# The product with V issued as two products of 256 queries, one behind each half of an attention slot, where another slot follows

## The chip, the cores and the metric

One core of one Trainium2 chip runs the whole program. The metric is the device time of one execution in microseconds; lower is better. The kernel before took 3469.8 us, the median of three runs between 3466.66 and 3474.9 us. Engines: TensorE (PE, its weight loads PEld), VectorE (DVE), ScalarE (ACT), GpSimd (POOL), SyncE (SP, which issues the DMAs).

## The reference

Four transformer-like layers follow each other on `x` of 4 batches x 1024 rows x 256 features, all in float32. What matters here is the self-attention of layer 0 and of layer 2, with 16 heads of 16 features:

```
s = einsum('bqhd,bkhd->bhqk', q, k) * scale      # layer 0: masked by blocks; layer 2: all keys
a = softmax(s, axis=-1)
out = einsum('bhqk,bkhd->bqhd', a, v)
```

Layers 0 and 2 go on with an output projection, cross attention over 77 context rows and an MLP; layer 1 is a mixture of three experts, layer 3 another cross attention, computed together with layer 2.

## The kernel before

Two program regions hold a self-attention: `FEWR` for layer 0 (two key tiles of 128 matter, so `per` = 2; a general region `GENR` is built beside it and not run with these inputs) and `L2R` for layer 2 (`per` = 8 key tiles). A region works on blocks: one block is one batch `b`, one group `g` of four heads (`j` = 0 to 3, one in each 32 rows of the array) and one half `qh` of the queries (512). There are 32 blocks in a region: 64 slots in layer 0 and 256 in layer 2.

A **slot** is one step of that pipeline for one key tile. For slot `t`, TensorE's program (`slot`, line 1149) has two halves, and each half has, before the change:

- the scores of slot `t` for two heads, written to two PSUM banks (`("sc", t, j)`: heads 0 and 1 in the first half, 2 and 3 in the second). In layer 2 (`by_parts`) a score takes three matmuls of 512 columns on 32 rows of the array: two parts of q, and the row of subtracted maxima (`max_rows`);
- the *fills*: scores of a later block, the other way round, for the other two heads, into two more banks, from which VectorE takes the maxima (`max_halves`, L1680). Heads 2 and 3 in the first half, 0 and 1 in the second, so that the four groups of 32 rows are all in use;
- behind the first half alone, the product with V of slot `t`-1 (`pv`, line 1099): four matmuls of 512 columns, 128 rows x 32 array columns each, that accumulate over a block's key tiles in the bank `ACC`. It waits for all four exponentials of slot `t`-1. Below, a slot's product is numbered by its key tile `i` (0 to 7 in layer 2).

The trace and the instruction order name a matmul `ps<-moving,stationary`: `ps<-q_blocks,k_groups` are the score parts, `ps<-max_rows,max_rows_ones` their third step, `ps<-k_groups,q_blocks` the fills, `ps<-big,probs` the product with V (a float32 matmul is two instructions in the trace, one in the order).

ScalarE turns each score bank into exponentials (L2024, `big<-ps`), and with that frees the bank. Seven banks form a **ring** (`take`, `R.freed`): the scores, fills and transposes take them in the order in which TensorE's program names them, and TensorE waits until the engine that reads the bank's entry seven places earlier has freed it. A slot takes 8 (four scores, four fills), so the fill of head 3 in the next slot's first half gets the bank of this slot's score of head 2.

Once in a block, behind a slot's second half, come four transposes of maxima (`nms`, L1180; in layer 2 in the slot whose product is `i` = 5) and four of the accumulated output (`tails`, L1168; in the slot whose product is `i` = 0). The product with `i` = 0 starts a new sum in `ACC`, and so first waits until ScalarE has copied the old one out (`R.acc`, L1999, `o_T<-ps`).

A planner (`overlapped`) puts the slots and all other work of the layer (projections, cross attention, MLP) into one order, by costs and due times worked out when the program is built. That order is fixed, and every engine keeps it. In layer 2's first 200 us hardly anything but slots is ready; later a slot usually has other matmuls on both sides.

Of the kernel before, what the change touches and what calls it, by code (L numbers as in the profile page):

```python
# [16 lines left out]
NB, SEQ, D = 4, 1024, 256  # L17
# [5 lines left out]
HALF = 512  # L23
# [42 lines left out]
def pixart_kernel(nc, io):  # L66
    ctx = ExitStack()
    with ctx:
# [51 lines left out]
        PS = ctx.enter_context(nc.psum_tensor("ps", [P, 8, HALF], F32))  # L120
# [11 lines left out]
        PB = BIG[:, 8192:12288].rearrange("p (a j n) -> p a j n", a=2, j=HG)  # L132
# [138 lines left out]
        ACC = 7  # L271

        class Region:
# [3 lines left out]
            def __init__(self, name, l, few, overlap, rows_first):  # L277
                self.name, self.l, self.few, self.rope, self.masked = name, l, few, l == 0, l == 0 and not few
                self.keys = list(range(NT - LIVE, NT)) if few else list(range(NT))
                self.per = len(self.keys)  # L280
                self.total = NG * NH * self.per
                self.split = l == 2
                self.lead = self.per + (3 if self.split else 2)
                self.rows_first = rows_first
                self.crosses = (1,) if l == 0 else (1, 2)
                self.share = 12.0 if few else 3.4
                self.order = overlapped(self) if overlap else sequential(self)
                self.number, self.lns, self.turns, self.loads, self.adds = {}, {}, [], {}, {}
                self.parted = [tok[1:] for tok in self.order if tok[0] == "qk"] if self.split else []
                self.cross_products = [tok for tok in self.order if tok[0] == "cp"]  # L290
                self.kv_users = [tok[2:] for tok in self.order if tok[0] == "load" and tok[1] == "k"]
                self.last = {}
                for tok in self.order:
                    if tok[0] in ("oP", "cp"):
                        self.last[tok[:3]] = tok
                    elif tok[0] == "m2":
                        self.last[tok[:2]] = tok
                self.cross_outs = [tok for tok in self.order if tok[0] == "ct"]
                n = 0
                for tok in self.order:  # L300
                    for key in self.entries(tok):
                        self.number[key] = n
                        n += 1
                    if tok[0] == "lnA":
                        self.lns[tok[1:]] = len(self.lns)
                    if tok[0] == "qk" and self.rope:
                        self.turns.append(tok[1:])
                    if tok[0] == "load":
                        self.loads[tok[1:]] = sum(1 for k in self.loads if k[0] == tok[1])
                    for add in self.bias_adds(tok):  # L310
                        self.adds[add] = len(self.adds)
                self.ring_full, self.ring_free = (sems(name + side, "0 1 2 3 4 5 6") for side in ("ring_full", "ring_free"))
                self.pv, self.acc, self.nm, self.rec, self.crec = sems(name, "pv_done acc_out max_done recip cross_recip")
                self.ln_st, self.ln_mv, self.ln_ep, self.ln_rs, self.ln_norm = sems(name + "ln_", "stats mean_var eps rstd rows")
                if not self.split:
                    self.rp_f, self.qe, self.ke = sems(name, "turned groups_act groups_dve")
                    self.x_in, self.x_g, self.cs, self.ones = sems(name, "wco_in wco_gated cos_sin_in v_ones")
                else:
                    self.ba_g = sems(name, "bias_o_gated")[0]
                    self.part_hi, self.nm_f, self.nm_h = sems(name, "part_hi max_f32 max_hi")  # L320
                    self.part_out = sems(name, "parts_out_0 parts_out_1")
                    self.q_in = sems(name, "q_block_in_0 q_block_in_1 q_block_in_2")
                    self.kg_in = sems(name, "k_group_in_0 k_group_in_1")
                self.xt = XTP if overlap else XT
                if few:
                    self.t12, self.fr, self.cos, self.sin = KE[:, 0:2, 0:HALF], KE[:, 2:4, 0:HALF], VS[:, 1152:1664], VS[:, 1664:2176]
                else:
                    pairs = PR[:, 0:2048].rearrange("p (x a n) -> p x a n", x=2, a=2)
                    self.t12, self.fr, self.cos, self.sin = pairs[:, 0], pairs[:, 1], OT[:, 0:HALF], OT[:, HALF:SEQ]
                self.affine = (0, 1, 2, None) if l == 0 else (4, 5, 6, 7)  # L330
                self.eps = (1e-5, 1e-5, 1e-5, None) if l == 0 else (1e-6, 1e-6, 1e-6, 1e-5)
                self.o_in, self.o_g, self.m_in, self.m_g, self.w1_in = sems(name, "wo_in wo_gated w2_in w2_gated w1_in")
                self.k_in = sems(name, "kv_in_first kv_in_second")
                self.bm_g, self.biased = sems(name, "bias_m_gated biased")
# [639 lines left out]
        def _(pe):  # L974
            def mm(out, lhsT, rhs, first=True, last=True):
                return pe.matmul(out, lhsT, rhs, start=first, stop=last)  # L976
# [3 lines left out]
            for kt in range(KT):  # L980
                last = pe.transpose(PS[:, 0, kt * NB:(kt + 1) * NB], condR[:, kt * P:(kt + 1) * P], ident[0:NB, 0:NB])
# [72 lines left out]
            def region_pe(R):  # L1054
# [41 lines left out]
                                last = mm(PS[:, bank, q * P:(q + 1) * P], MQ[:, qh * 4 + q, kt * P:(kt + 1) * P], bigI[:, :], False, q == 3)  # L1096
                        done(last, ("sc", t, j))

                def pv(t):
                    b, g, qh, i = R.at(t)  # L1100
                    for j in range(HG):
                        pe.wait_ge(*R.freed(("sc", t, j)))
                    if i == 0:
                        if t:
                            pe.wait_ge(R.acc, t // R.per)
                        if R.few:
                            pe.wait_ge(*R.freed(("v", b, 0, 0)))
                        else:
                            for k in range(2):
                                pe.wait_ge(*R.freed(("v", b, g // 2, k)))  # L1110
                    for j in range(HG):
                        h = 8 * (g // 2) + 2 * j + g % 2
                        last = mm(PS[32 * j:32 * j + 32, ACC, :], R.v_tile(b, i, h), PB[:, t % 2, j, :], i == 0, i == R.per - 1)
                    last.then_inc(R.pv, 1)

                def by_parts(t, f, half):
                    keys, stationary, moving = [], [], []
# [30 lines left out]

                def slot(tok):
                    _, score, fills, product, tails, nms = tok  # L1150
                    for half in range(2):
                        if R.split:
                            by_parts(score, fills, half)
                            if half == 0 and product is not None:
                                pv(product)
                            continue
                        if score is not None:
                            scores(score, half)
                        for key in R.fills(fills, half):
                            fill(key)  # L1160
                        if half == 0 and product is not None:
                            pv(product)
                    for q in tails:
                        pe.wait_ge(R.acc, q + 1)
                        bank = take(("tail", q))
                        for i in range(4):
                            c = (q % 2) * HALF + i * P
                            last = pe.transpose(PS[:, bank, i * P:(i + 1) * P], OT[:, c:c + P], ident[:, :])  # L1168
                        done(last, ("tail", q))
                    for q in nms:  # L1170
                        if R.few:
                            pe.wait_ge(*R.freed(("max", q, R.per - 1, 1)))
                        else:
                            pe.wait_ge(R.nm, q + 1)
                        b, g, qh = R.block(q)
                        bank = take(("nm", q))
                        for i in range(4):
                            qt = 4 * qh + i
                            rows = NM[:, q % 2, i:i + P] if R.split else NM[:, 2 * qh + g % 2, qt:qt + P]
                            last = pe.transpose(PS[:, bank, i * P:(i + 1) * P], rows, ident[:, :])  # L1180
                        done(last, ("nm", q))
# [17 lines left out]
                for tok in R.order:  # L1199
# [5 lines left out]
                    elif kind == "v":  # L1205
                        b, m = tok[1:]
                        for hf in range(NH):
                            wait_turned("lnT", 0, b, hf)
                        for i in range(1 if R.few else 2):
# [5 lines left out]
                            else:  # L1215
                                for u in range(4):
                                    t = 4 * i + u
# [1084 lines left out]
```

## Time and profile before

| | us |
|---|---|
| median of three runs | 3469.8 |
| the profiled execution | 3466.48 |
| its span on the core | 3464.7 |
| PE busy in the span | 3150.7 (91%) |
| DVE busy | 1823.9 (53%) |
| ACT busy | 1464.3 (42%) |

The span is the time from the first to the last instruction; 1.8 us of the execution lie around it. Matmuls on different rows or columns of the array overlap, so PE's busy time is the time in which at least one was under way, and a matmul's duration runs on while the next has already begun. The distance between starts is therefore what the sums below use. Idle time is written in brackets behind a row, with the instruction whose end closed it.

### The profile page before, as it was taken

How to read it: one execution, taken by the hardware profiler on the slowest of the kernel's cores; microseconds unless marked ns; L12 is line 12 of the kernel's file. 1: busy time of each engine (PE TensorE's matmuls, PEld its weight loads, DVE VectorE, ACT ScalarE, POOL GpSimd, SP SyncE). 2: the span in 40 equal slices, each digit the busy share in tenths (PEclk: the TensorE clock that was granted, in tenths of full speed). 3: DMA queues.
4: the chain of work that ended last, by engine and by line, in shares of the span. 5: the costliest groups of instructions: out<-in, count | busy, mean ns of one | idle time of the engine just before them, and what ended most of it. 6: DMA issues, size and time to landing. Idle time of an engine off the chain costs nothing.

```text
span 3464.7 us, 51568 instructions
## 1 busy us (share of the span) xinstructions
PE 3150.7 (91%) x20564; PEld 1858.1 (54%) x20564; DVE 1823.9 (53%) x3812; ACT 1464.3 (42%) x2645; POOL 257.2 (7%) x278
## 2 busy tenths in 40 slices
PE   6899999999889999998488989999999999999887
PEld 3555666656576656665234445454454545554464
DVE  4876554562412332323377765757757577557343
ACT  0343444444312222221046645555456555565433
POOL 1100010010100000000100001001100101001010
PEclk9998999999889999999689989999999999999899
DMA  5200000003000000000420020001200000000000
GB/s 168 91 1 6 8 21 1 15 14 96 16 23 0 1 0 1 1 0 5 143 67 32 26 75 24 15 20 44 86 13 22 28 28 25 13 28 31 1 1 13
DMA packets 78707, 104.29 MB, mean 30 GB/s; under 512 B 18688, under 2 KB 52208, under 8 KB 78204
## 3 DMA queue, kind: packets, MB, share of 16 engines
q1 hardware_dynamic: 78468, 100.93, 9.0%
q8 instruction: 171, 2.80, 0.3%
q14 instruction: 68, 0.56, 0.1%
HBM read 72.05 MB, written 28.86 MB: 29 GB/s over the span
## 4 chain that ended last, share of the span: by engine, by line
PE 80%; DVE 9%; ACT 4%; DMA 2%; issue 2%; SPq 1%; POOL 1%; DVEq 0%; ACTq 0%; POOLq 0%
PE ps L976 73%; PE ps L1189 3%; DVE max_halves L1680 2%; ACT big L2024 2%; DMA k_parts<-qk_parts 1%; PE ps L1316 1%; PE ps L1180 1%; DVE row_max_cross L1846 1%; DMA q_parts<-qk_parts 1%; PE ps L1168 1%; DVE xn_tok L1752 1%; DVE bn_stats L1716 1%; ACT probs L2083 1%; SPq L877 1%; DVE bn_stats L1739 1%
## 5 line engine op out<-in xcount | busy, mean ns | idle before, releaser
L2024 ACT ACTIVATE big<-ps 128x512 f32<-128x512 f32 x1280 | 692.7, 595 | 668.3 <-PE ps L976 667.8
L1680 DVE TENSOR_REDUCE max_halves<-ps 128x1 f32<-128x512 f32 x1024 | 650.3, 683 | 239.9 <-PE ps L976 232.4
L976 PE MATMUL ps<-k_groups,q_blocks 32*128 32x512 f32 x2048 | 449.4, 464 | 89.8 <-DVE qk_parts L1815 33.8
L976 PE MATMUL ps<-q_blocks,k_groups 32*128 32x512 f32 x2048 | 423.4, 468 | 4.0 <-DVE qk_parts L1815 2.0
L976 PE MATMUL ps<-big,probs 128*32 128x512 f32 (+1 forms) x2688 | 383.6, 613 | 12.3 <-ACT big L2024 5.8
L976 PE MATMUL ps<-weights_mlp,big 128*128 128x256 f32 (+1 forms) x1248 | 333.5, 419 | 2.5 <-ACT big L2095 2.5
L976 PEld LDWEIGHTS ps<-q_blocks,k_groups 32*128 32x128 f32 x2048 | 175.9, 187 | 297.2 <-issue 282.9
L976 PEld LDWEIGHTS ps<-weights_mlp,big 128*128 128x128 f32 x1248 | 234.0, 190 | 83.6 <-issue 57.9
L976 PEld LDWEIGHTS ps<-k_groups,q_blocks 32*128 32x128 f32 x2048 | 188.8, 190 | 158.4 <-ACT big L2024 55.6
L1722 DVE TENSOR_TENSOR x_tok<-ps,x_tok 128x512 f32<-128x512 f32 x112 | 77.2, 690 | 312.1 <-PE ps L976 311.9
L2083 ACT ACTIVATE probs<-ps 77x512 f32<-77x512 f32 x384 | 196.2, 591 | 96.0 <-PE ps L976 95.7
L976 PE MATMUL ps<-x_T,weights_mlp 128*128 128x256 f32 x1024 | 231.4, 385 | 2.3 <-ACT x_T L2046 2.3
L976 PE MATMUL ps<-big 32*128 32x256 f32 (+2 forms) x1664 | 224.3, 492 | 10.0 <-DVE row_max L1677 4.3
L1677 DVE TENSOR_REDUCE row_max<-ps 128x2 f32<-128x512 f32 x256 | 164.6, 684 | 103.3 <-PE ps L976 103.1
L976 PEld LDWEIGHTS ps<-x_T,weights_mlp 128*128 128x128 f32 x1024 | 195.3, 193 | 34.6 <-ACT x_T L2046 4.9
L976 PE MATMUL ps<-max_rows,max_rows_ones 32*128 32x512 f32 x1024 | 204.5, 398 | 0.0
L976 PEld LDWEIGHTS ps<-big 32*128 32x128 f32 (+1 forms) x1664 | 142.3, 193 | 108.6 <-issue 80.6
L976 PE MATMUL ps<-weights,x_T 128*128 128x256 f32 x640 | 164.9, 412 | 2.9 <-ACT x_T L1999 2.9
L1846 DVE TENSOR_REDUCE row_max_cross<-ps 128x4 f32<-128x308 f32 x384 | 155.0, 469 | 17.2 <-PE ps L976 16.0
L2095 ACT ACTIVATE big<-ps,mlp_b 128x256 f32<-128x256 f32 x256 | 106.8, 470 | 128.0 <-PE ps L976 127.8
L976 PE MATMUL ps<-big,k_v_cross 32*77 32x512 f32 (+1 forms) x832 | 156.0, 627 | 3.2 <-DVE big L1852 2.2
L2238 POOL TENSOR_SCALAR eps_tile<-mean_var 128x4 f32<-128x4 f32 x56 | 13.3, 237 | 1845.4 <-DVE mean_var L1745 1845.3
(233 smaller groups left out, 3970.7 us busy)
## 6 DMA issues: line engine op xcount, KB each, us to landing
q_blocks<-q_parts SPq DMA_DIRECT2D x64, 256.0 KB
q_parts<-qk_parts SPq DMA_DIRECT2D x48, 256.0 KB
k_parts<-qk_parts SPq DMA_DIRECT2D x32, 256.0 KB
k_groups<-k_parts SPq DMA_DIRECT2D x16, 512.0 KB
weights_mlp<-in_L_xcond_mlp_W SPq DMA_DIRECT2D x5, 1024.0 KB, 5.3
weights_mlp<-in_L_xcond_W_mlp SPq DMA_DIRECT2D x5, 1024.0 KB, 5.1
x_tok<-in_x SPq DMA_DIRECT2D x4, 1024.0 KB, 9.6
out_y<-x_tok SPq DMA_DIRECT2D x8, 512.0 KB, 3.2
```

Of the source, the lines that this page charges most:

```text
L877: sp.dma_start(dst, STG[:, n % STAGES, part, :].bitcast(F32)).then_inc(R.part_out[n % STAGES], 16)
L976: return pe.matmul(out, lhsT, rhs, start=first, stop=last)
L1168: last = pe.transpose(PS[:, bank, i * P:(i + 1) * P], OT[:, c:c + P], ident[:, :])
L1180: last = pe.transpose(PS[:, bank, i * P:(i + 1) * P], rows, ident[:, :])
L1189: last = pe.transpose(PS[:, banks[ft], (t % 4) * P:(t % 4 + 1) * P], rows[:, t, ft * P:(ft + 1) * P], ident[:, :])
L1677: dve.tensor_reduce(NM[:, 2 * qh + e, c:c + 2], PS[:, bank, :].rearrange("p (t n) -> p t n", t=2), AX.X, ALU.max, negate=True).then_inc(R. ...
L1680: dve.tensor_reduce(NMP[:, e, j, qt, hf:hf + 1], PS[:, bank, :], AX.X, ALU.max, negate=True).then_inc(R.frees(key), 1)
L1722: dve.tensor_tensor(x, PS[:, R.bank(key), :], x, ALU.add).then_inc(R.frees(key), 1)
L1846: dve.tensor_reduce(dst, src, AX.X, ALU.max, negate=True).then_inc(R.frees(key), 1)
L2024: act.activation(PB[:, score % 2, j, :], PS[:, R.bank(key), :], ACT.Exp, scale=SCALE).then_inc(R.frees(key), 1)
L2083: act.activation(PC[0:NC, j, :], PS[0:NC, R.bank(key), :], ACT.Exp, scale=SCALE).then_inc(R.frees(key), 1)
L2095: last = act.activation(HT[hf][:, m, :], PS[:, R.bank(key), i % 2 * D:(i % 2 + 1) * D], ACT.Gelu_apprx_tanh, bias=B1[:, 0 if R.l == 0 else ...
```

## The change

In `Region.__init__` the set `followed` collects the slots behind which the fixed order places another slot directly (tokens that cost TensorE nothing are skipped). In such a slot, if its product isn't the block's first (`product % R.per > 0`), `slot` now issues the product as two: queries 0 to 255 behind the first half's scores and fills, queries 256 to 511 behind the second half's. Each has four matmuls of 256 columns with the same weights. The signal that a product is done (`R.pv`) and the end of a block's sum go with the second. All other slots keep the one product of 512.

```
--- before.py
+++ after.py
@@ -288,6 +288,8 @@
                 self.number, self.lns, self.turns, self.loads, self.adds = {}, {}, [], {}, {}
                 self.parted = [tok[1:] for tok in self.order if tok[0] == "qk"] if self.split else []
                 self.cross_products = [tok for tok in self.order if tok[0] == "cp"]
+                placed = [tok for tok in self.order if cost(self, tok)]
+                self.followed = {tok for tok, after in zip(placed, placed[1:]) if tok[0] == after[0] == "slot"}
                 self.kv_users = [tok[2:] for tok in self.order if tok[0] == "load" and tok[1] == "k"]
                 self.last = {}
                 for tok in self.order:
@@ -1096,7 +1098,7 @@
                                 last = mm(PS[:, bank, q * P:(q + 1) * P], MQ[:, qh * 4 + q, kt * P:(kt + 1) * P], bigI[:, :], False, q == 3)
                         done(last, ("sc", t, j))
 
-                def pv(t):
+                def pv(t, columns, closes):
                     b, g, qh, i = R.at(t)
                     for j in range(HG):
                         pe.wait_ge(*R.freed(("sc", t, j)))
@@ -1110,8 +1112,9 @@
                                 pe.wait_ge(*R.freed(("v", b, g // 2, k)))
                     for j in range(HG):
                         h = 8 * (g // 2) + 2 * j + g % 2
-                        last = mm(PS[32 * j:32 * j + 32, ACC, :], R.v_tile(b, i, h), PB[:, t % 2, j, :], i == 0, i == R.per - 1)
-                    last.then_inc(R.pv, 1)
+                        last = mm(PS[32 * j:32 * j + 32, ACC, columns], R.v_tile(b, i, h), PB[:, t % 2, j, columns], i == 0, closes and i == R.per - 1)
+                    if closes:
+                        last.then_inc(R.pv, 1)
 
                 def by_parts(t, f, half):
                     keys, stationary, moving = [], [], []
@@ -1148,18 +1151,19 @@
 
                 def slot(tok):
                     _, score, fills, product, tails, nms = tok
+                    halved = tok in R.followed and product is not None and product % R.per > 0
                     for half in range(2):
                         if R.split:
                             by_parts(score, fills, half)
-                            if half == 0 and product is not None:
-                                pv(product)
-                            continue
-                        if score is not None:
-                            scores(score, half)
-                        for key in R.fills(fills, half):
-                            fill(key)
-                        if half == 0 and product is not None:
-                            pv(product)
+                        else:
+                            if score is not None:
+                                scores(score, half)
+                            for key in R.fills(fills, half):
+                                fill(key)
+                        if halved:
+                            pv(product, slice(half * D, half * D + D), half == 1)
+                        elif product is not None and half == 0:
+                            pv(product, slice(0, HALF), True)
                     for q in tails:
                         pe.wait_ge(R.acc, q + 1)
                         bank = take(("tail", q))
```

74 of the 320 slots that run are concerned: 6 in layer 0 (products 3, 5, 7, 9, 11, 13 of its 64), and 68 in layer 2 (numbered 0 to 255): 48 in the first stretch (1 to 30 and 33 to 55, without the products with `i` = 0), six pairs (59 and 60, 110 and 111, 124 and 125, 171 and 172, 187 and 188, 228 and 229) and 242 to 247, 251 and 252 at the end, where no fills are left. The order on VectorE, ScalarE, GpSimd and SyncE is the same as before.

TensorE in layer 2, from product 1 (`big,probs`) to product 2, before: the second half of one slot (five rows), then directly the first half of the next (five rows).

```order
L976 MATMUL ps<-big,probs 32x512 x4
L976 MATMUL ps<-q_blocks,k_groups 128x512 x2
L976 MATMUL ps<-k_groups,q_blocks 128x512 x2
L976 MATMUL ps<-q_blocks,k_groups 128x512 x2
L976 MATMUL ps<-k_groups,q_blocks 128x512 x2
L976 MATMUL ps<-max_rows,max_rows_ones 128x512 x2
L976 MATMUL ps<-q_blocks,k_groups 128x512 x2
L976 MATMUL ps<-k_groups,q_blocks 128x512 x2
L976 MATMUL ps<-q_blocks,k_groups 128x512 x2
L976 MATMUL ps<-k_groups,q_blocks 128x512 x2
L976 MATMUL ps<-max_rows,max_rows_ones 128x512 x2
L976 MATMUL ps<-big,probs 32x512 x4
```

And now; the last five rows are again the next slot's first half, behind which product 2's first part comes.

```order
L978 MATMUL ps<-big,probs 32x256 x4
L978 MATMUL ps<-q_blocks,k_groups 128x512 x2
L978 MATMUL ps<-k_groups,q_blocks 128x512 x2
L978 MATMUL ps<-q_blocks,k_groups 128x512 x2
L978 MATMUL ps<-k_groups,q_blocks 128x512 x2
L978 MATMUL ps<-max_rows,max_rows_ones 128x512 x2
L978 MATMUL ps<-big,probs 32x256 x4
L978 MATMUL ps<-q_blocks,k_groups 128x512 x2
L978 MATMUL ps<-k_groups,q_blocks 128x512 x2
L978 MATMUL ps<-q_blocks,k_groups 128x512 x2
L978 MATMUL ps<-k_groups,q_blocks 128x512 x2
L978 MATMUL ps<-max_rows,max_rows_ones 128x512 x2
```

Half of the product has moved behind the second half's matmuls, between them and the next slot's first scores.

TensorE in layer 0, from product 3 to product 4 (`big` 128x512 the scores, 128x256 the fills, `row_max` the transposes of maxima), before:

```order
L976 MATMUL ps<-big,probs 32x512 x4
L976 MATMUL ps<-big 128x512 x2
L976 MATMUL ps<-big 128x256 x4
L1180 MATMUL ps<-ident,row_max 128x128 x4
L976 MATMUL ps<-big 128x512 x2
L976 MATMUL ps<-big 128x256 x4
L976 MATMUL ps<-big,probs 32x512 x4
```

And now:

```order
L978 MATMUL ps<-big,probs 32x256 x4
L978 MATMUL ps<-big 128x512 x2
L978 MATMUL ps<-big 128x256 x4
L978 MATMUL ps<-big,probs 32x256 x4
L1184 MATMUL ps<-ident,row_max 128x128 x4
L978 MATMUL ps<-big 128x512 x2
L978 MATMUL ps<-big 128x256 x4
L978 MATMUL ps<-big,probs 32x512 x4
```

Here the moved part stands between the second half and the four transposes.

## Rows read from the trace of the kernel before

**Rows 1.** The page: engines' busy time, and the chain that ended last by engine.

```profile
PE 3150.7 (91%) x20564; PEld 1858.1 (54%) x20564; DVE 1823.9 (53%) x3812; ACT 1464.3 (42%) x2645; POOL 257.2 (7%) x278
PE 80%; DVE 9%; ACT 4%; DMA 2%; issue 2%; SPq 1%; POOL 1%; DVEq 0%; ACTq 0%; POOLq 0%
```

**Rows 2.** The chain in layer 2's first stretch (start us, us, what).

```profile
1813.58 0.61 ACT big L2024
1814.19 0.04 issue
1814.23 2.65 PE ps L976 x23
...
1816.90 0.61 ACT big L2024
```

**Rows 3.** Waits of PE, 1780 to 1980 us (total us, times, longest).

```profile
PE ps L976 <- ACT big L2024: 18.1, 40, 0.5
```

**Rows 4.** Timeline of one slot (start us, us, what, idle before).

```profile
1851.07 0.50 PE L976 MATMUL ps<-q_blocks,k_groups 32*128 32x512 f32 x2
...
1851.64 0.40 PE L976 MATMUL ps<-max_rows,max_rows_ones 32*128 32x512 f32 x2
...
1851.65 0.39 PE L976 MATMUL ps<-q_blocks,k_groups 32*128 32x512 f32 x2
1851.85 2.71 DVE L1680 TENSOR_REDUCE max_halves<-ps 128x1 f32<-128x512 f32 x4 [0.60 <-PE ps L976]
...
1852.07 1.08 ACT L2024 ACTIVATE big<-ps 128x512 f32<-128x512 f32 x2 [0.71 <-PE ps L976]
...
1852.72 0.49 PE L976 MATMUL ps<-k_groups,q_blocks 32*128 32x512 f32 x1 [0.45 <-ACT big L2024]
...
1853.39 1.07 PE L976 MATMUL ps<-big,probs 128*32 128x512 f32 x8
...
1854.38 0.50 PE L976 MATMUL ps<-q_blocks,k_groups 32*128 32x512 f32 x2
```

**Rows 5.** Timeline where the transposes of maxima follow (products 21 and 22).

```profile
1847.27 0.50 PE L976 MATMUL ps<-q_blocks,k_groups 32*128 32x512 f32 x2
...
1848.18 0.66 PE L1180 MATMUL ps<-ident,row_max 128*128 128x128 f32 x4
...
1848.76 0.50 PE L976 MATMUL ps<-q_blocks,k_groups 32*128 32x512 f32 x2
...
1850.07 1.07 PE L976 MATMUL ps<-big,probs 128*32 128x512 f32 x8
```

**Rows 6.** Timeline where a block ends (product 24 waits for `o_T`).

```profile
1856.35 0.61 ACT L1999 ACTIVATE o_T<-ps 128x512 f32<-128x512 f32 x1
...
1857.32 1.07 PE L976 MATMUL ps<-big,probs 128*32 128x512 f32 x8 [0.56 <-ACT o_T L1999]
```

**Rows 7.** Groups of PE by shape (count, busy us, mean ns).

```profile
L976 PE MATMUL ps<-big,probs 128*32 128x512 f32 x2560 | 353.2, 624 | 11.8 <-ACT big L2024 5.8 <-ACT o_T L1999 5.3 <-DVE max_halves L1680 0.5
...
L976 PE MATMUL ps<-weights_mlp,big 128*128 128x256 f32 x1024 | 228.0, 381 | 2.5 <-ACT big L2095 2.5
...
L976 PE MATMUL ps<-weights_mlp,big 128*128 128x512 f32 x224 | 105.5, 592 | 0.0
```

**Rows 8.** Layer 0, timeline of PE from product 9's second half on.

```profile
193.05 1.15 PE L976 MATMUL ps<-big 32*128 32x512 f32 x12
194.13 0.66 PE L1180 MATMUL ps<-ident,row_max 128*128 128x128 f32 x4
...
196.40 0.64 PE L976 MATMUL ps<-big,probs 128*32 128x512 f32 x4
```

**Rows 9.** Layer 2's end, no fills: products 244 and 245.

```profile
3205.55 1.07 PE L976 MATMUL ps<-big,probs 128*32 128x512 f32 x8 [0.80 <-ACT big L2024]
...
3208.78 0.64 PE L976 MATMUL ps<-big,probs 128*32 128x512 f32 x4 [1.25 <-ACT big L2024]
```

**Rows 10.** Busy us of each engine, 1776 to 1976 us, granted clock behind POOL.

```profile
1776.00:1976.00 200.00, 178.19 (x1662) 76.58 (x1656) 150.99 (x249) 128.61 (x239) 2.94 (x14) 1.00 0.10 35
```

## The prediction

> **What bounds the kernel now.** I read the page's busy times and chain first. TensorE is busy 91% of the span and holds 80% of the chain, VectorE 53% and 9% [rows 1]: what counts is where TensorE itself waits inside the slots. The chain in layer 2's first stretch shows that wait as a cycle: 2.65 us of matmuls, then one 0.61 us exponential, with period 1816.90 - 1813.58 = 3.32 us, one slot [rows 2]. TensorE's waits give the amount, 18.1 us in 40 waits of 0.45 on `big` from ScalarE [rows 3]. The timeline of one slot says why [rows 4]. With the start of a slot's second half (1851.07) as zero:
>
> - its third score step starts at 0.57, and the next slot's first half follows at 0.58, beside it;
> - ScalarE begins the exponential of head 2's score at 1.00, as soon as that is complete;
> - at 1.65 the bank comes free, and the fill of head 3, which takes that bank, starts behind 0.45 us of idle. The other matmuls of the half are queued behind it;
> - the product starts at 2.32 (0.67 later) and holds TensorE for 0.99, until the next second half at 3.31.
>
> So between second half and product 1.74 us pass, with little to do before the bank is free, while the product comes only after that. ScalarE itself is not full: it sat idle 0.71 before that exponential, and VectorE 0.60 before its maxima [rows 4]; over 200 us of this stretch they are busy 128.6 and 151.0 us [rows 10].
>
> **The change part by part.** It adds, in 74 slots, four matmuls of 256 columns with their loads and the repeated waits, and moves half of the product behind the second half.
>
> *A half product.* The trace has no product of 256 columns. A float32 matmul of 256 columns takes 381 ns against 592 for 512 on the full array [rows 7], so 256 columns are worth 0.21 per pass; the product has two passes in which its four matmuls overlap, and 0.99 - 2 x 0.21 = 0.57. Bounds: 0.50 (exactly half) and 0.99 (no column saved). I take 0.57, since the product's own mean of 624 ns lies by the 592 of the same width.
>
> *The lost overlap.* Scores can't start beside the third step any more when a product stands between. From a second half's start to transposes behind it 1848.18 - 1847.27 = 0.91 pass [rows 5], against 0.58 to a next half; I take 0.91 before each half product. The step before the product fits it: 0.67 after the late fill, of which two steps. The second part's repeated waits were met before the first part, and lie in that same 0.91.
>
> *The plain slot.* Second half and half product 0.91 + 0.57 = 1.48; then the next first half starts. Its fourth matmul needs the bank freed at 1.65, 0.17 later. A first step is followed by the second after 1.65 - 1.48 + 0.67 = 0.84 at most until the product, less than the 0.91 that the half takes anyway, so the wait is absorbed. The same holds for the other half, whose last fill needs head 0's exponential: the distances are the same. A slot lasts 2 x 1.48 = 2.96 instead of 3.31: 0.35 less. ScalarE's two pairs (1.08 each) fit. VectorE's four maxima, 2.71 with the last one's end [rows 4], fit less easily; they are the first cover to go (below).
>
> *The slots at a block's ends.* Before the slot with `i` = 1 stands an unhalved one; only its own first part is shorter: 0.42. Behind the halved `i` = 5 come the transposes, 1848.76 - 1848.18 = 0.58, which filled the wait already; from second half to product it was 1850.07 - 1847.27 = 2.80 [rows 5], so 3.79 with the product. Now 0.91 + 0.57 + 0.58 + 0.91 + 0.57 = 3.54: 0.25 less. Behind `i` = 7, the next product waits for ScalarE's copy of the sum: 1857.32 - 1854.38 = 2.94 after the second half [rows 4, 6]. Now TensorE is there after 0.91 + 0.57 + 0.91 = 2.39, and waits as long as before. The copy itself comes behind four exponentials, at 1.97 [rows 6], when the second part, over at 1.48, is long done. So nothing is won or lost there. A block with seven halved slots gains 0.42 + 4 x 0.35 + 0.25 + 0.35 = 2.42.
>
> *The sum.* First stretch: six blocks of seven, 14.5, and one of six (0.42 + 1.40 + 0.25, less 0.07 as its last part stands before an unhalved product: 2.39 against 2.32), 2.0: 16.5. Six pairs: 0.42 + 0.35 each, 4.6; behind three an unhalved plain slot (0.07 each), behind two the transposes (2.97 against 2.80, 0.17 each), behind one a block's start: less 0.55, so 4.1. Slots without fills have period 3208.78 - 3205.55 = 3.23, bound by the exponentials that the product waits for, 1.25 of idle [rows 9]; now the matmuls' 2.96: eight slots, 2 x 0.42 + 6 x 0.27 - 0.07 = 2.4. Layer 0: a half slot takes 194.13 - 193.05 = 1.08, and second half to product 3.35 [rows 8]; with the part in it 1.08 + 0.57 + 0.58 + 1.08 = 3.31, hence 0.42 + 0.04 = 0.46, times six 2.8. Together 25.8, say 26 us. All of it lies on TensorE, and the order behind it is fixed.
>
> Nothing else is late: the maxima, the loads and ScalarE's order are untouched; the finished signal of a product moves back by 1.0 us or so, and the exponential that needs it (the buffer of two slots before) starts only after the next half is through.
>
> The profiled execution took 3466.5 (span 3464.7), 3.3 below the median; 3466.5 - 26 = 3440.5, and on the median's scale **3444 us**.
>
> A rule speaks against the change: the Trainium skill, TensorEngine Tiling (Array Packing), section Key Properties, says that changing the tiling mode drains TensorE, and scores (32 rows) and products (32 columns) are two modes. The trace agrees: 0.91 instead of 0.58 where another shape follows [rows 4, 5]. If those drains came on top, 74 x 0.33 = 24 us of the gain would go, by the rows; but most of each lies in the wait.
>
> **The rivals.**
>
> *The halves cost nearly what the whole did.* If the passes are set by the four column strips' loads and starts and not by columns, each half costs up to 0.99, a plain slot 2 x (0.91 + 0.99) = 3.80, and the change is slower. Some 140 half products lie on the path (those behind `i` = 7 are covered), 0.42 more each: 59 us, 26 - 59 = 33 us slower, **3503**. It decides from a half product of about 0.75 on, where 26 us are used up. For it: eight loads and starts are issued again, and nothing so narrow and short was profiled. Against: 256 columns save 0.21 in every full-array row [rows 7].
>
> *VectorE becomes the bound.* Four maxima need about 2.5 to 2.7 of a 2.96 slot, and once in a block the minima and the normalisation stand in between. If the banks then come late from VectorE, the slot stays at about 3.13 and half is won: 13 us, **3457**. For it: 151 of 200 us busy [rows 10]. Against: VectorE has a whole slot to free a bank, ScalarE half of one.
>
> *The stretch's gain is given back.* If what follows at 1976 waits for transfers or GpSimd rather than for TensorE, 16.5 us are lost and 9 stay: **3460**. Against: later stages' chain is TensorE as well [rows 1].
>
> That the change touches too little is no rival of its own: 74 slots are named by the order, and 18.1 us of idle stand in one stretch alone [rows 3].
>
> **How the numbers follow.** The forecast has 0.73, spread by the half product (0.50 gives 10 us more, 0.65 gives 12 less) between 3433 and 3457. VectorE as bound has 0.12, the gain given back 0.07, costly halves 0.08. About 0.2% (7 us) can be told from no change. Faster: 0.73 + 0.11 + 0.03 = 0.87. Same (a half near 0.75, or the weak ends of the others): 0.06. Slower: 0.07. The range 3431 to 3463 takes in the two weaker gains and leaves out the slower side and a few executions whose granted clock differs; in the first stretch that clock is 1.00, the 2.4 GHz level [rows 10].
>
> **What would show it.** In the changed kernel's groups `ps<-big,probs` splits into 246 x 8 = 1968 of 512 and 74 x 16 = 1184 of 256 columns, about 400 ns each. In the timeline a part is followed by the next half after 0.57, a plain slot lasts 2.96, products 1 to 55 take some 16 us less, and TensorE's waits on `big` in that stretch shrink to a few us, while those on `o_T` stay. Wrong would be: parts of 0.75 and more, waits on `max_halves` in the place of those on `big`, or slots shorter and the span not.

## The result, and the profile after

The changed kernel took 3441.47 us, the median of four runs between 3439.14 and 3451.98; the kernel before took 3472.35 beside them. The ratio is 0.9917 with a 95% interval of 0.9901 to 0.9933. Forecast were 3444 us, with 3431 to 3463 as the range. In a second session (`changed_again` below) it was 0.9934 [0.9916, 0.9952]. The execution profiled after is the longest of its four (3451.98, span 3450.2), so the stretches below are compared piece by piece, not by the spans.

From the page of the changed kernel, as in [rows 1]:

```profile
PE 3162.4 (92%) x21156; PEld 1867.7 (54%) x21156; DVE 1824.0 (53%) x3812; ACT 1467.0 (43%) x2645; POOL 256.9 (7%) x278
PE 80%; DVE 10%; DMA 3%; ACT 3%; issue 2%; SPq 1%; POOL 1%; DVEq 0%; ACTq 0%; POOLq 0%
```

There are 592 matmul instructions more, 74 x 8. TensorE is busy 11.7 us longer in a span 14.5 us shorter: it sits idle 26.2 us less, and 11.7 of that went into longer busy time (stretches at the lower clock are in it, in both kernels).

TensorE's waits in the changed kernel from 1780 to 1980 us (total us, times, longest), answering [rows 3]:

```profile
PE ps L978 <- ACT o_T L2003: 2.7, 5, 0.5
PE ps L978 <- DVE qk_parts L1819: 1.7, 2, 0.9
PE ps L978 <- DMA q_blocks<-q_parts: 1.0, 1, 1.0
PE ps L978 <- DVE max_halves L1684: 0.5, 1, 0.5
```

The 18.1 us in 40 waits on `big` are gone altogether. The wait on `o_T` at a block's end stays, as forecast. A wait on the load of `q_blocks` is new; those on `qk_parts`, in the slots of products 0 and 1, the kernel before has too, just ahead of this window. One slot of the changed kernel on the timeline, for [rows 4]:

```profile
1864.30 0.64 PE L978 MATMUL ps<-big,probs 128*32 128x256 f32 x8
...
1864.87 0.50 PE L978 MATMUL ps<-q_blocks,k_groups 32*128 32x512 f32 x2
...
1865.69 1.29 DVE L1684 TENSOR_REDUCE max_halves<-ps 128x1 f32<-128x512 f32 x2 [0.22 <-PE ps L978]
...
1865.81 0.64 PE L978 MATMUL ps<-big,probs 128*32 128x256 f32 x8
1865.94 1.09 ACT L2028 ACTIVATE big<-ps 128x512 f32<-128x512 f32 x2 [0.36 <-PE ps L978]
...
1866.38 0.50 PE L978 MATMUL ps<-q_blocks,k_groups 32*128 32x512 f32 x2
...
1867.16 1.29 DVE L1684 TENSOR_REDUCE max_halves<-ps 128x1 f32<-128x512 f32 x2 [0.18 <-PE ps L978]
...
1867.28 0.64 PE L978 MATMUL ps<-big,probs 128*32 128x256 f32 x8
```

Each part is followed by the next half after 0.57 (1864.87 - 1864.30; 1866.38 - 1865.81); between a half and its part 0.94 and 0.90 pass; from one first part to the next it is 1867.28 - 1864.30 = 2.98, and over the stretch's plain slots 2.94 to 2.98, but for products 19 (4.07) and 51 (3.07), of which more below. VectorE's idle in front of two maxima has shrunk to 0.18 and 0.22, but it is idle: here it does not bind.

TensorE in the changed kernel by shape (count, busy us, mean ns, idle before), for [rows 7]:

```profile
L978 PE MATMUL ps<-big,probs 128*32 128x512 f32 x1968 | 271.4, 624 | 4.5 <-ACT o_T L2003 3.8 <-DVE max_halves L1684 0.5
L978 PE MATMUL ps<-big,probs 128*32 128x256 f32 x1184 | 95.3, 394 | 0.0
```

The counts are the forecast ones, and a matmul of 256 columns takes 394 ns.

At the program's end the two kernels differ in the clock. Busy time, granted clock, DMA share and GB/s from 3180 to 3260 us, here of the kernel before:

```profile
3180.00:3260.00 80.00, 71.04 (x482) 33.67 (x483) 27.28 (x54) 43.66 (x81) 4.05 (x5) 0.87 0.04 10
```

The same of the changed kernel:

```profile
3180.00:3260.00 80.00, 75.05 (x625) 38.83 (x623) 37.19 (x83) 44.78 (x82) 7.27 (x8) 1.00 0.02 8
```

Before, 20.5 us of this stretch, from 3219.8 on, were granted the lower level (1.2 GHz); in the changed kernel, none. From one product's first matmul to another's, and with the clock's share, the time went as follows (profiled executions; "at half clock" is the length of the stretches with clock below 1.00 times what was missing of it):

| stretch | before | half clock | changed | half clock | changed_again | half clock |
|---|---|---|---|---|---|---|
| start to layer 0's product 0 | 141.2 | 15.4 | 142.8 | 18.8 | 142.8 | 18.8 |
| layer 0, products 0 to 17 | 105.8 | 1.7 | 110.0 | 6.8 | 108.7 | 5.1 |
| to layer 2's product 0 | 1521.5 | 93.9 | 1524.7 | 97.3 | 1518.2 | 92.2 |
| layer 2, products 0 to 56 (first stretch) | 203.7 | 0.0 | 189.2 | 0.0 | 188.6 | 0.0 |
| products 56 to 241 (with the pairs) | 1220.3 | 30.7 | 1217.8 | 29.0 | 1221.4 | 32.4 |
| products 241 to 255 (end) | 65.5 | 10.2 | 54.1 | 0.0 | 54.1 | 0.0 |
| to the end of the span | 206.6 | 11.9 | 211.7 | 22.2 | 214.5 | 24.8 |

The first stretch and the end carry the gain. Layer 0 lost time, the pairs gave hardly any, and the long rows move by a few us either way with the clock that they got. The 206.6 us at the end of the kernel before is the shortest of all ten profiles (the others have 210.0 to 215.9, `in_place` with the same order there 215.9), so that row can't be put down to the change.

### The profile page after: what moved, and what is told of

It is laid out like the page before. It is cut to its first block, busy times and chain, and to the rows that moved or that the text cites. A ratio compares the mean times of both kernels' runs of the same rounds, so it can differ in the third digit from the quotient of the medians.

```text
span 3450.2 us, 52900 instructions
## 1 busy us (share of the span) xinstructions
PE 3162.4 (92%) x21156; PEld 1867.7 (54%) x21156; DVE 1824.0 (53%) x3812; ACT 1467.0 (43%) x2645; POOL 256.9 (7%) x278
## 4 chain that ended last, share of the span: by engine, by line
PE 80%; DVE 10%; DMA 3%; ACT 3%; issue 2%; SPq 1%; POOL 1%; DVEq 0%; ACTq 0%; POOLq 0%
PE ps L978 73%; PE ps L1193 3%; DVE max_halves L1684 2%; DMA k_parts<-qk_parts 1%; PE ps L1320 1%; PE ps L1184 1%; DVE row_max_cross L1850 1%; DMA q_parts<-qk_parts 1%; PE ps L1172 1%; ACT big L2028 1%; ACT probs L2087 1%; DVE bn_stats L1720 1%; DMA q_blocks<-q_parts 1%; DVE xn_tok L1756 1%; SPq L879 1%
## 5 line engine op out<-in xcount | busy, mean ns | idle before, releaser
L978 PE MATMUL ps<-big,probs 128*32 128x512 f32 (+2 forms) x3280 | 397.1, 531 | 5.0 <-ACT o_T L2003 3.8
L978 PEld LDWEIGHTS ps<-k_groups,q_blocks 32*128 32x128 f32 x2048 | 197.6, 189 | 120.9 <-DVE qk_parts L1819 39.0
L978 PEld LDWEIGHTS ps<-big,probs 128*32 128x32 f32 (+1 forms) x3280 | 87.3, 112 | 157.3 <-issue 126.4
```

## The experiments

The theory (A): TensorE's wait on a bank inside the slot goes, because half a product fills it. Its rivals: the product's place behind the second half matters and not its halving, or the two parts cost something by themselves, and the gain's places are others than the sum says. First the two halves of the edit alone, in all 74 slots.

**The whole product behind the second half** (`moved_whole`).

```
 if halved:
-    pv(product, slice(half * D, half * D + D), half == 1)
+    if half == 1:
+        pv(product, slice(0, HALF), True)
```

> In the same 74 slots the product stays one of 512 queries, and stands as a whole behind the second half. Theory A (the cycle: each half must wait for an exponential that the half before it released; the product has to be shared between both gaps): the wait moves to the other gap, where no product stands any more. A plain slot stays at 0.58 + 1.07 of waiting + 0.67 + 0.99 = 3.31 us, and the time within 5 us of the kernel before. Theory B (it is enough that some matmuls stand between a second half and the next slot's scores): most of the gain is kept, 20 us or more less than before, and plain slots near 2.9 us.

Measured: 3460.23 us, ratio 0.9965 [0.9951, 0.9979]. TensorE in a plain slot:

```profile
1793.87 1.07 PE L978 MATMUL ps<-big,probs 128*32 128x512 f32 x8
1794.86 0.50 PE L978 MATMUL ps<-q_blocks,k_groups 32*128 32x512 f32 x2
...
1796.57 0.49 PE L978 MATMUL ps<-k_groups,q_blocks 32*128 32x512 f32 x1 [0.52 <-ACT big L2029]
...
1797.23 0.64 PE L978 MATMUL ps<-big,probs 128*32 128x512 f32 x4
```

The wait is back (0.52, now in the half with no product in it), the slot is 1797.23 - 1793.87 = 3.36, and the first stretch is 205.2 against 203.7. So the place alone wins nothing there, as theory A had it. The time, 12 us below the kernel before, lies outside its "within 5 us", though: what the place does win is the end, 50.3 against 65.5, where a plain slot without fills takes 2.35. I had not expected that.

**Two parts, but both behind the first half** (`in_place`).

```
 if halved:
-    pv(product, slice(half * D, half * D + D), half == 1)
+    for part in range(2 if half == 0 else 0):
+        pv(product, slice(part * D, part * D + D), part == 1)
```

> In the same 74 slots the product is two of 256 queries, but both stand behind the first half. Theory A: nothing fills the wait, and the second product costs what two parts of 0.57 take more than one of 0.99, 0.15 us: a plain slot of 3.46 us, 74 x 0.15 = 11 us slower than before. Theory B (shorter products are themselves the gain, since their end comes earlier): no slower than before. Theory C (a product of 256 columns costs what it does through its loads and starts, and its 0.57 in the changed kernel contains work hidden beside scores): 0.8 us and more for a part that stands behind another, over 30 us slower.

Measured: 3471.96 us, ratio 1.0002 [0.999, 1.0014]. TensorE:

```profile
1852.28 1.07 PE L978 MATMUL ps<-big,probs 128*32 128x256 f32 x16
1853.28 0.50 PE L978 MATMUL ps<-q_blocks,k_groups 32*128 32x512 f32 x2
```

Two parts in sequence hold TensorE for 1.00, as the whole did for 0.99 [rows 4]: the additional loads and starts cost nothing that shows. My expectation of 11 us more had taken 0.57 twice. Nor is the halving by itself a gain: products 0 to 56 take 203.7, as before. From 1.00 for two and 0.57 for one, a part is 0.43 and the end of a product, before another shape starts, 0.14.

**Where the gain is: the first stretch alone, layer 0 alone, the end alone.** Each takes the changed kernel with one more condition on `halved`:

```
-halved = tok in R.followed and product is not None and product % R.per > 0
first_stretch, 48 slots:
+halved = tok in R.followed and product is not None and product % R.per > 0 and R.l == 2 and product < 56
layer0, 6 slots:
+halved = tok in R.followed and product is not None and product % R.per > 0 and R.l == 0
end_only, 8 slots:
+halved = tok in R.followed and product is not None and product % R.per > 0 and R.l == 2 and product > 241
```

> Only the 48 slots of layer 2's first stretch are halved (products 1 to 55); layer 0, the six pairs and the slots without fills keep the one product. Theory A by the sum of the prediction: 16 us less than before, plain slots of 2.96 us, and the end of the program as far from the stretch as before. Theory B (the changed kernel won as much outside the stretch, by the clock of the end above all): 16 us or less of the 29, with the half-clock stretch of some 20 us near product 248 in the profile as in the kernel before.

Measured: 3453.48, ratio 0.995 [0.9933, 0.9968], which is 17.4 us of 3472; products 0 to 56 took 188.2. This term of the sum was 16.5.

> Only the 6 slots of layer 0 are halved. By the prediction's sum 2.8 us less than before, which this measurement can hardly tell from none. Rival: products 5 and 13, whose second half waits 0.82 instead of 0.39 us for an exponential in the changed kernel and is followed there by a stretch at half clock that the kernel before does not have, cost 2.1 us each: the profile then shows both stretches again, products 3, 7, 9 and 11 at 3.92 instead of 4.35 us, and the time lies 1 to 3 us above the kernel before or level with it.

Measured: 3478.8, ratio 1.0018 [1.0006, 1.003]: slower, by 6 us. Its products 0 to 17 take 105.6 us, 0.2 less than before, so no more than that is won where the edit is. The rest lies later, where its kernel is that of before: its first stretch took 207.8 (3.4 of that is clock), products 56 to 241 1223.3. The half-clock stretches at products 5 and 13 that the rival expected are not in this profile; the two slots take 0.57 more each without them. Over its runs the mean granted clock is 0.948 against 0.950. Why six altered slots should be followed by a lower clock later is open.

> Only the eight slots without fills at the end of layer 2 are halved (products 242 to 247, 251, 252). Theory A (two effects: each slot 0.27 us shorter, and, because TensorE idles less there, the granted clock stays at the 2.4 GHz level near product 248, where the kernels without a moved product had some 20 us at half clock in the profile): 8 to 13 us less than before, products 248 to 251 some 9 us closer together, mean clock some 0.002 to 0.003 higher. Theory B (the half-clock stretch came and went by chance): 2 to 3 us less than before, and the stretch is there.

Measured: 3453.41, ratio 0.9946 [0.9931, 0.996], which is 18.7 us (16.4 between the medians), more than the 8 to 13 expected; products 241 to 255 took 54.0 against 65.5, and no half clock is in them. The gain of the work that I had put at 2.4 is 2.1 here: six of the eight slots take 2.93 to 2.95 instead of 3.22 to 3.31; those of products 245, where transposes follow, and 247 take 3.51 and 3.50 instead of 3.37 and 3.93. TensorE in them, for [rows 9]:

```profile
3201.44 0.64 PE L978 MATMUL ps<-big,probs 128*32 128x256 f32 x8
3202.00 0.73 PE L978 MATMUL ps<-q_blocks,k_groups 32*128 32x512 f32 x4
3202.58 0.39 PE L978 MATMUL ps<-max_rows,max_rows_ones 32*128 32x512 f32 x2
3202.90 0.64 PE L978 MATMUL ps<-big,probs 128*32 128x256 f32 x8
```

No bracket is left where [rows 9] have 0.80 and 1.25 of idle. Behind the last of these slots, where product 248 waits for the copy of the sum, 0.51 is left of what was, in the kernel before:

```profile
3219.30 1.47 PE L976 MATMUL ps<-big,probs 128*32 128x512 f32 x8 [1.95 <-ACT o_T L1999]
```

The other 9.4 us are the slots behind: products 248 to 251 took 5.59 + 6.91 + 10.48 = 22.98 before and 3.37 + 3.81 + 6.44 = 13.62 now. Those slots are unaltered, and before they ran at the lower clock. In four of the ten profiles the slots from product 242 on keep their waits (before, `in_place`, `first_stretch`, `layer0`): TensorE sits idle 5.7 us between products 241 and 248, and all four have this stretch, 17 to 20.5 us at half clock between 3197 and 3250, which begins 0.3 to 1.7 us after product 248 does. In the six with shorter slots TensorE sits idle 0.5 to 2.4 us there, and none has the stretch. The two with the whole product behind keep waits, but short ones; from `moved_whole`:

```profile
PE ps L978 <- ACT big L2029: 1.6, 4, 0.5
PE ps L978 <- ACT o_T L2004: 0.7, 1, 0.7
```

So in these profiles the idle time need not be gone, only less. Which of the waits counts, no run takes apart.

**Layer 0's products 5 and 13 left whole** (`without_5_13`), since the trace after showed them longer.

```
-halved = tok in R.followed and product is not None and product % R.per > 0
+halved = tok in R.followed and product is not None and product % R.per > 0 and (R.l == 2 or product not in (5, 13))
```

> The changed kernel, but in layer 0 products 5 and 13 are whole; there the second part stood 0.57 us of matmuls on top of a wait that had only moved. Theory A: 1 to 2 us less at the same clock than the changed kernel, and no half-clock stretches behind products 5 and 13, so 2 to 6 us less in all: 3437 to 3441. Theory B (layer 0's halves cost nothing that lasts): level with the changed kernel.

Measured: 3440.94, ratio 0.9912 [0.9897, 0.9928], against 3447.65 for the changed kernel on the same chip. That is the 2 to 6 us less of theory A and a little more, mostly with the clock: by the fit in the next section it is about 1 us at an equal clock. Products 0 to 17 took 104.5 instead of 108.7, with 1.7 instead of 5.1 lost to the clock. The two times' runs overlap by a hair (3435.79 to 3446.24 against 3444.01 to 3456.56).

**Each place with what suits it** (`first_and_end`): halves in the first stretch, the whole product behind the second half in the end's eight slots, layer 0 and the pairs as before.

```
+halved, behind = halved and R.l == 2 and product < 56, halved and R.l == 2 and product > 241
...
-elif product is not None and half == 0:
+elif product is not None and half == behind:
```

> A version made of what the runs so far say: the 48 slots of the first stretch are halved, the eight slots without fills have the whole product behind the second half (2.35 instead of 2.93 us a slot in the run with whole products moved), layer 0 and the six pairs are as before the change. Theory A: 17 us from the stretch, some 5 from the end's slots, some 8 from the end's clock: 3438 to 3443, and below the changed kernel by what layer 0's halves cost, 2 to 6 us. Theory B (the gains share one source, the idle of TensorE, and don't add): 3446 or more.

Measured: 3440.94, ratio 0.9911 [0.9895, 0.9927]; the lowest run of all, 3431.87, is one of its. Products 241 to 255 took 50.3, though the first of them 7.91 instead of 6.43. TensorE in a slot without fills there:

```profile
3184.77 0.75 PE L978 MATMUL ps<-q_blocks,k_groups 32*128 32x512 f32 x8
...
3185.68 1.06 PE L978 MATMUL ps<-big,probs 128*32 128x512 f32 x8
```

With no product in between, the scores of both halves, four heads, run beside each other in 3185.68 - 3184.77 = 0.91; in `end_only` above, two heads take 3202.90 - 3202.00 = 0.90 by themselves. By the medians it is 6.7 us below the changed kernel and level with `without_5_13`, with 56 altered slots instead of 72.

**The changed kernel once more** (`changed_again`), on that chip.

> The changed kernel once more, beside the others on one chip. Theory A (29 us less, of which some 21 are work and waits at the same clock and 8 are clock): 3440 to 3446, with a mean granted clock of 0.953 or more. Theory B (the four runs so far had a good clock by chance): 3448 to 3454 with a mean clock of 0.950 as in the kernel before.

Measured: 3447.65, ratio 0.9934 [0.9916, 0.9952], with a mean granted clock of 0.951: between the two theories' times, and nearer to the second. Added up by their ratios, -17.4 (first stretch), -18.7 (end) and +6.2 (layer 0) make -29.9; measured were -28.8 at first and -22.9 here. So the parts account for the whole, within what repeats differ by, and leave the pairs no share that could be seen.

## Why the prediction was right, and where its sum was not

*The bound, the slot and its parts: right.* TensorE waited for banks behind ScalarE; 0.57 and 0.91 were measured as 0.57 and 0.90 to 0.94, 2.96 as 2.94 to 2.98. Where the transposes follow, 3.54 was worked out and 3.53 to 3.55 measured in six of seven slots (product 37's took 3.82, against 3.80 before). Before a new sum nothing was to be won, and the row that answers [rows 6] shows the same wait:

```profile
1860.50 1.07 PE L978 MATMUL ps<-big,probs 128*32 128x512 f32 x8 [0.54 <-ACT o_T L2003]
```

A whole block, from the product with `i` = 0 to the next, came down from 1829.26 - 1801.17 = 28.09 to 1833.72 - 1808.01 = 25.71: 2.38 less, where 2.42 was forecast. The stretch's 16.5 came as 14.5 in this profile, 15.5 in `first_stretch`'s and 17.4 in its times. Of the 2.0 missing in the first, 1.1 is one load that the shorter slots ran into (the rest lies at products 1, which waits for `qk_parts` as before, 37 and 51):

```profile
1846.62 0.49 PE L978 MATMUL ps<-q_blocks,k_groups 32*128 32x512 f32 x2 [1.03 <-DMA q_blocks<-q_parts]
```

That slot took 4.07; in three other profiles with halved slots it took 3.11 to 3.31, in `first_stretch` 2.96. In `first_and_end` product 51's slot has such a wait and takes 4.06. "Nothing else is late: the maxima, the loads and ScalarE's order are untouched" was thus not quite true: the load is untouched, but its cover became shorter.

*Costly halves: wrong, as given.* The parts' price is by columns (`in_place`). The Trainium skill, TensorEngine Tiling (Array Packing), section Key Properties, says that a change of tiling mode drains TensorE. These runs agree: two parts in one mode cost nothing extra, and a part with scores on both sides 0.14 at its end beside the 0.33 in front. The plain slot had idle time for both: 0.45 on the bank before, none now.

*The six pairs: mis-sized, 4.1 forecast and some 0.7 measured.* Here the rival "VectorE becomes the bound" was right for the first slot of each pair. Around products 59 and 60 in the changed kernel, VectorE and TensorE's loads:

```profile
1980.54 1.39 DVE L1720 BATCH_NORM_STATS2 bn_stats<-x_tok 128x6 f32<-128x256 f32 x4
...
1981.97 0.38 DVE L1749 BATCH_NORM_AGGREGATE mean_var<-bn_stats 128x2 f32<-128x6 f32 x4
...
1982.27 2.45 DVE L1684 TENSOR_REDUCE max_halves<-ps 128x1 f32<-128x512 f32 x4
...
1983.58 0.18 PEld L978 LDWEIGHTS ps<-k_groups,q_blocks 32*128 32x128 f32 x2 [0.42 <-DVE max_halves L1684]
```

The four maxima stand behind 1.77 us of normalisation, and the fill waits for their bank. All six pairs have these rows in the changed kernel, and their first interval is 3.52 to 3.53 in both kernels. VectorE had bound it before: in the kernel before, each of the six has a wait like this one:

```profile
1988.54 0.49 PE L976 MATMUL ps<-q_blocks,k_groups 32*128 32x512 f32 x1 [0.29 <-DVE max_halves L1680]
```
Of the second intervals one stays (3.31, 3.29), three gain 0.32, 0.21 and 0.21, and two fall from 3.31 to 3.01 or 3.02, but what follows takes 0.3 longer there (6.35 to 6.64, 6.40 to 6.71). There the transposes of maxima wait for GpSimd's `row_max`, at the first of the two before and then in the changed kernel:

```profile
2764.00 0.66 PE L1180 MATMUL ps<-ident,row_max 128*128 128x128 f32 x4 [2.04 <-POOL row_max L2224]
```

```profile
2755.98 0.66 PE L1184 MATMUL ps<-ident,row_max 128*128 128x128 f32 x4 [2.32 <-POOL row_max L2228]
```

That is the third rival, on a small scale: the gain is given back at the next wait for another engine. For the first stretch it was wrong, since `first_stretch` kept its 15.5 us (17.4 in its times). The step took the plain slot's price from a stretch with VectorE 0.60 idle in each slot to places where VectorE has other work; no row of these places stood under it.

*Layer 0: mis-sized, 2.8 forecast, 0.2 measured alone and a loss with the clock.* "0.42 + 0.04 = 0.46, times six" holds for products 3, 9 and 11 (4.35 to 3.92) and half for 7 (4.35 to 4.10). Products 5 and 13 have another wait behind their second half's first scores. TensorE in `layer0`, where no half clock is near:

```profile
169.15 0.64 PE L978 MATMUL ps<-big,probs 128*32 128x256 f32 x8
169.72 1.14 PE L978 MATMUL ps<-big 32*128 32x512 f32 x8
171.68 1.13 PE L978 MATMUL ps<-big 32*128 32x256 f32 x4 [0.82 <-ACT big L2028]
172.73 0.64 PE L978 MATMUL ps<-big,probs 128*32 128x256 f32 x8
173.30 0.66 PE L1184 MATMUL ps<-ident,row_max 128*128 128x128 f32 x4
```

And in `without_5_13`, with that product whole:

```profile
168.07 0.61 PE L978 MATMUL ps<-big,probs 128*32 128x512 f32 x4
168.62 1.14 PE L978 MATMUL ps<-big 32*128 32x512 f32 x8
170.15 1.13 PE L978 MATMUL ps<-big 32*128 32x256 f32 x4 [0.40 <-ACT big L2028]
171.21 0.66 PE L1184 MATMUL ps<-ident,row_max 128*128 128x128 f32 x4
```

ScalarE frees that bank at its own time. The shorter first part only lengthens the wait for it (0.40 to 0.82), and the second part comes behind the wait, with its 0.57 in full: 5.25 to 5.82. I had read the layer's price from product 9 [rows 8] and multiplied. In the two profiles of the changed kernel a stretch at half clock also falls on one or both of these slots (7.34 and 7.39; 5.82 and 7.05).

*The end: the work right, its effect not.* 2.4 was forecast and 2.1 measured as work; the 9.4 us of clock behind it were not thought of. The prediction's "executions whose granted clock differs" took the clock for chance, while here it came with the idle time in front: in all four profiles that have the 5.7 us, in none of the six with less.

*The total* is right partly by luck, since errors cancelled: 3.4 us too much for the pairs and 2.6 to 7 for layer 0, against 9 (by the profiles) to 16 (by `end_only`'s times) too little at the end. Over the 110 executions of the nine kernels, fitted with one level for each kernel and one common slope on the mean granted clock, time falls by 2.4 us for each 0.001 of clock. At an equal 0.950 the changed kernel is 20.6 us below the one before (3452.2 against 3472.8); the rest of its 23 to 29 us comes with the clock, 0.9522 against 0.9503 over their runs. That fit separates the two by arithmetic; only the stretch behind the no-fill slots is shown by an edit.

*Still open*: why the nine later profiles show 25 to 36 us at half clock in the last 60 us of the span, where the one of before has 14, and how far that is chance. In the window from 3400 to 3450 us (granted clock third from the end) the changed kernel has:

```profile
3400.00:3450.00 50.00, 34.95 (x196) 17.18 (x193) 17.47 (x37) 11.97 (x23) 0.00 (x0) 0.69 0.06 22
```

`first_stretch` and `layer0`, whose end is ordered as before, have such stretches too, so it is not the halves at the end that bring them.

## What to carry to other kernels

Where a matmul engine waits inside a pipeline's step for a bank that another engine frees, cut the work that comes after the wait and put a part of it in front; the gain can be computed from one slot's timeline, and moving that work whole only moves the wait. That price holds only where the same engine ends the wait: look at one row for each place in which the edit applies, above all where a part would come behind a wait that is not shortened, and leave those places as they are. And look at what runs behind idle time on TensorE, and at which clock: here a few waits of 1 to 2 us became shorter, and the unaltered work behind them ran at 2.4 GHz instead of 1.2.

## What was not expected of the hardware

- The lower clock can follow from waits in the order itself: with 5.7 us of idle in 26.7 (waits of 0.45 to 1.95 us, among them the 0.80 and 1.25 of [rows 9]), 17 to 20.5 us behind them were granted 1.2 GHz in each of four profiles; with 0.5 to 2.4 us of idle in their place, none in six. TensorE was itself busy 22.7 of the 23 us from 3219 to 3242 while the clock was low.
- Four matmuls on 32 array columns each, twice with 256 moving columns, take as long as once with 512 (1.00 and 0.99), although loads and starts double.
- A product of 512 at the end of a slot without fills, behind the second half, gives 2.35 to 2.36 in a plain slot, against 2.93 with the two parts and 3.23 with the whole behind the first half. Without fills the scores of all four heads take 0.91 beside each other, and those of two heads alone 0.90: a part put between the halves takes that overlap away.
